# Attention epilogue two groups behind instead of one, and two constant loads issued by ScalarE

## The reference

```python
q1, k1, q2, k2, v = (heads(x @ w.T) for w in (q1_w, k1_w, q2_w, k2_w, v_w))
attn1 = softmax(q1 @ k1.T / sqrt(128));  attn2 = softmax(q2 @ k2.T / sqrt(128))
o = (attn1 - lam * attn2) @ v                      # per head, lam is one number for a head
x = layernorm(x + merge_heads(o) @ o_w.T)
scale = max(absmax(x, per token), 1e-7) / 127;  q = clip(round(x / scale), -128, 127)
f = (q @ weight.T) * scale * w_scale + bias        # weight is int8; f is rounded to f16
out = layernorm(x + f)
```

## Time and profile before

| | us |
|---|---|
| median of 3 runs (3500.14 to 3505.44) | 3500.18 |
| the profiled execution's own time | 3496.5 |
| its span, slowest core (core 4) | 3495.0 |
| spans of the 8 cores | 3478.9 to 3495.0 |
| attention block, about | 0 to 2864 |
| output projection block, about | 2865 to 3195 |
| FFN block, about | 3195 to 3495 |

### The profile page before, as it was taken

The page is one execution under the profiler, slowest core; times in us unless marked ns, Lnnn a source line. Parts: engine busy times, 40 slices in busy tenths (PEclk is TensorE's granted clock), DMA queues, the critical chain, the costliest instruction groups (busy, mean ns, idle before and its releaser), DMA issues. The chain is left out here.

```text
span 3495.0 us, 44882 instructions; the slowest of 8 cores (3478.9 to 3495.0 us)
## 1 busy us (share of the span) xinstructions
PE 3029.3 (87%) x16387; PEld 1385.5 (40%) x16640; DVE 1278.8 (37%) x1521; ACT 1268.4 (36%) x1283; POOL 36.0 (1%) x72
## 2 busy tenths in 40 slices
PE   1973999999999999898999999999999968883897
PEld 1432343434343535353535344444434323441343
DVE  0121333332323232424233323243333334774476
ACT  0250343443435251616171616152534342331222
POOL 0000000000000000000000000000000000000000
PEclk9996999999999999999999999999999988996898
DMA  9653101010101010101011010101000014443343
GB/s 149 146 175 107 34 4 34 4 34 4 34 4 35 3 35 2 35 3 36 12 27 27 11 32 5 32 6 32 6 3 5 4 61 143 122 120 115 103 123 111
DMA packets 98707, 172.79 MB, mean 49 GB/s; under 512 B 73664, under 2 KB 73664, under 8 KB 92096
## 3 DMA queue, kind: packets, MB, share of 16 engines
q0 software_dynamic: 11280, 75.50, 10.6%
q1 hardware_dynamic: 87216, 94.41, 8.6%
HBM read 174.07 MB, written 50.33 MB: 64 GB/s over the span
## 5 line engine op out<-in xcount | busy, mean ns | idle before, releaser
L279 ACT ACTIVATE pb<-psA 128x1024 bf16<-128x1024 f32 x512 | 524.2, 1024 | 1378.5 <-PE psA L243 1378.5
L261 PE MATMUL pS<-pb,ones 128*128 128x512 bf16 x2000 | 601.3, 380 | 2.5
L279 ACT ACTIVATE pb<-psB 128x1024 bf16<-128x1024 f32 x512 | 524.3, 1024 | 134.6 <-PE psB L243 134.6
L257 PE MATMUL pO<-pb,vv 128*128 128x512 bf16 x1008 | 381.1, 378 | 127.2 <-ACT pb L279 115.9
L43 DVE RECIPROCAL r<-sc_ 128x512 f32<-128x512 f32 x128 | 429.1, 3353 | 102.2 <-DMA osc<-oout 88.2
L225 PE MATMUL psB<-xTb,wq 128*128 128x512 bf16 x2000 | 460.4, 379 | 2.5
L225 PE MATMUL psA<-xTb,wq 128*128 128x512 bf16 x2000 | 457.8, 379 | 2.7 <-issue 0.2
L43 DVE COPY sc_<-pS 128x1024 f32<-128x1024 f32 x64 | 78.4, 1224 | 902.9 <-PE pS L261 902.8
L257 PE MATMUL pO<-pb,v 128*128 128x512 bf16 x1024 | 388.0, 379 | 3.7 <-issue 3.6
L243 PE MATMUL psA<-q,k 128*128 128x512 bf16 x992 | 299.9, 381 | 19.6 <-DVE k L43 17.9
L257 PEld LDWEIGHTS pO<-pb,vv 128*128 128x128 bf16 x1024 | 98.4, 96 | 517.0 <-issue 508.8
(11 more groups left out here) (73 smaller groups left out, 1734.7 us busy)
## 6 DMA issues: line engine op xcount, KB each, us to landing
wq<-wqkv POOLq DMA_DIRECT2D x16, 2560.0 KB, 16.5
xin<-x SPq DMA_DIRECT2D x16, 1024.0 KB, 5.3
out<-oo SPq DMA_DIRECT2D x16, 1024.0 KB, 5.3
xTb<-xT POOLq DMA_DIRECT2D x1, 8192.0 KB, 55.0
stg<-wo POOLq DMA_DIRECT2D x16, 512.0 KB, 6.7
wob<-stg SPq DMA_DIRECT2D x16, 512.0 KB, 2.7
stg<-wffn POOLq DMA_DIRECT2D x16, 512.0 KB, 4.7
wfb<-stg SPq DMA_DIRECT2D x16, 512.0 KB, 2.9
```

The lines of the kernel that those rows point to most:

```text
L257: te.matmul(pO[:, j * 512:(j + 1) * 512], vv[:, cc * 128:(cc + 1) * 128], pslc, start=(cc == 0), stop=(cc == NC_ - 1))
L261: mm = te.matmul(pS[:, j * 512:(j + 1) * 512], ones_sb[:], pslc, start=(cc == 0), stop=(cc == NC_ - 1))
L279: sc.activation(pb_sb[:, (c % 2) * 1024:(c % 2) * 1024 + 1024], sbank[c % 2][:], AF.Exp, scale=INV_SQRT_HD,).then_inc(sEXP, 1)
```

## The change

oc and sc_ get three parts of 1024 columns instead of two. In the loop over groups VectorE runs `divide(grp - 2)` where it ran `divide(grp - 1)`, and both last divides come behind the loop. ScalarE's copy to oc waits for the divide of three groups before instead of two. oout keeps its two halves, and the wait on sODMA inside `divide` is as it was. In the FFN block the loads of wsb_sb and bb_sb, with the wait between them, go from SP's queue to the front of ScalarE's, whose first load waits for the end of the output projection's matmuls (sAR).

```diff
-            oc_sb = Eb(nc.sbuf_tensor("oc", [128, 2048], F32))
-            sc_sb = Eb(nc.sbuf_tensor("sc_", [128, 2048], F32))
+            oc_sb = Eb(nc.sbuf_tensor("oc", [128, 3072], F32))
+            sc_sb = Eb(nc.sbuf_tensor("sc_", [128, 3072], F32))
...
-                    if grp >= 2:
-                        sc.wait_ge(sCB, grp - 1)
-                    sc.copy(oc_sb[:, (grp % 2) * 1024:(grp % 2) * 1024 + 1024],
+                    if grp >= 3:
+                        sc.wait_ge(sCB, grp - 2)
+                    sc.copy(oc_sb[:, (grp % 3) * 1024:(grp % 3) * 1024 + 1024],
...
                 def divide(g2):
-                    b2 = (g2 % 2) * 1024
+                    b2 = (g2 % 3) * 1024
                     ve.wait_ge(sOC2, g2 + 1)
                     if g2 >= 2:
                         ve.wait_ge(sODMA, 64 * (g2 - 1))
...
                         grp = h * QT + qt
-                        if grp >= 1:
-                            divide(grp - 1)
+                        if grp >= 2:
+                            divide(grp - 2)
                         ve.wait_ge(sPVD, NC_ * (grp + 1))
-                        b = (grp % 2) * 1024
+                        if grp >= 3:
+                            ve.wait_ge(sCB, grp - 2)
+                        b = (grp % 3) * 1024
                         ve.tensor_copy(sc_sb[:, b:b + 1024], pS[:], inc=(sOC, 1, grp + 1))
+                divide(H * QT - 2)
                 divide(H * QT - 1)
...
                     sy.wait_ge(sTRE, 2 * NT)
-                    sy.wait_ge(sAUX, 16)
-                    sy.dma_start(out=wsb_sb[:], in_=wsb_d).then_inc(sAUX, 16)
-                    sy.wait_ge(sAUX, 32)
-                    sy.dma_start(out=bb_sb[:], in_=bb_d).then_inc(sAUX, 16)
                     sy.wait_ge(sCS, 32 * NC_)
...
                 def _(sc):
+                    sc.wait_ge(sAR, 2 * NT)
+                    sc.wait_ge(sAUX, 16)
+                    sc.dma_start(out=wsb_sb[:], in_=wsb_d).then_inc(sAUX, 16)
+                    sc.wait_ge(sAUX, 32)
+                    sc.dma_start(out=bb_sb[:], in_=bb_d).then_inc(sAUX, 16)
```

## The result

The changed kernel takes 3436.8 us (median of 8 runs, 3435.3 to 3438.9). Its ratio to the kernel before is 0.982, 95% interval 0.981 to 0.983. The forecast was 3429, range 3420 to 3439: right in sign and inside the range, 7.8 us too low.

A forecast was written before the change was run, and what follows sets the result against it. TensorE was taken as the bound, stalled once through VectorE's wait on oout's writes. Core 7: 3420.5 without the stall, + 9.3 tail - 4.0 loads = 3425.8; with 1.5 beyond the span and about half of 3.7, 3429 us, range 3420 to 3439.

The forecast's parts named there:

- Part 1: Attention, divide two groups behind: VectorE's stall on group 0's writes goes, 78.2 us on core 4, 67.8 on core 7.
- The slack rule: Attention, behind divide(2): writes of oout could come 21 us late before TensorE noticed, 5.7 us ahead plus 15.28 idle.
- The 61 waits: Attention, ScalarE's copy of pO: with the cover gone, waits of some hundredths of a microsecond, 1 to 3 us together.
- Part 2: End of attention: two divides instead of one behind the last group, nothing hides the second, +9.3 us.
- Part 3: FFN block start: wsb_sb and bb_sb on ScalarE's queue let wfsb start earlier, gain 4.0 us, ends 0.6 and 6.8.
- What I added for the median: Whole kernel: about half of the 3.7 us by which the median of runs exceeded the profiled one.
- 3.4 us for the loads: Upward range term, FFN block: the loads get in each other's way fully, gaining 0.6 us instead of 4.0.
- The 3 us for issue: Upward range term, attention: up to 3 us if ScalarE's waits for older divides cost issue time.
- A: FFN block: loads get in each other's way fully, gain only 0.6 us, time 3432; chance 0.12.
- B: Attention, group 4: the wait returns because writes land later; 40 us late leaves a 19 us stall, 3448; chance 0.04.
- C: Attention: TensorE's stall stays because something else, such as the weights, is late too; 3505 us; chance 0.02.
- D: Attention: slower, since without the stall's rest the granted clock falls; at 0.96 the time is 3531; chance 0.02.

The follow-up runs named there:

- the experiment on late writes: The changed kernel with eight more chunks (first 8 of the FFN weight again) staged ahead of the writes of oout: 3469.6 to 3470.5 us.

## Why the prediction was right, and by how much it was not

- **Part 1 is shown.** The stall was one wait on two reused halves of oout: it is gone with the lag, and just as much with four parts and no lag. Its price, 78.2 us on core 4 with the slow clock behind it and 65 to 72 on the others, was right to within 0.4 us in the block's mean. The slack rule (a late divide costs only what exceeds the idle time behind it) held in the experiment on late writes. There the slack behind the divide measured 15.0 us, where the prediction had 15.28; the rest of its 21 us is the margin ahead of the divide. The 61 waits that might have cost 1 to 3 us leave no trace in this mean.
- **Part 2 is shown.** The tail costs 9.3 us on the timeline, and attention ends 10.6 us apart in the two kernels that differ in it. The change gives back about a seventh of what it gains here, and four parts of oout do not.
- **Part 3 had the right sign and the wrong size.** The step that failed is "One more megabyte beside it costs 2.8: gain 6.8 - 2.8 = 4.0 us". Both terms were off. The 6.8 was core 4's; the eight cores had 5.4 to 7.1, mean 6.1. And the price of the extra megabyte was above 2.8: parts 0 and 1 together took 13.2 us in the mean, 3.7 more than before (part 0 took 6.2 to 8.1, where 5 to 6 was forecast). So the last part landed 2.0 us earlier in the mean (63.1 us after the block's start, 65.2 before). Core 4 went from 66.0 to 63.2, but core 7, from which the forecast was summed, from 63.9 to 64.4. The rest of the block was another 0.6 longer. The measured gain is 1.1 to 2.4 us. The Trainium skill (DMA: Bandwidth & Descriptors, "Issuing engines are not separate DMA queues") has the transfers share the same DMA engines whatever engine issues them, and only the time to issue is saved. As the prediction worked it out, that rule gives about 0.6 us; the traces lie between it and my sum.
- **The output projection block was taken as constant.** The prediction worked out each core's time by sliding the rest of its timeline, and so put this block's growth at nothing, for which it gave no reason. It measured +3.6 us in the mean: 1.4 up to the first tile's last sum and 2.0 in the 15 distances between tiles, both places where TensorE waits for loads. Sorted by kernel, the mean of the block is 334.0 to 336.1 us in the four profiles with the lag that leave this block alone, and 331.6 to 332.4 in the four without it. The cores of the kernels with four parts enter as close together as those of the lag alone, so the growth goes with the lag and not with their nearness. It is one profile for each kernel, a pattern and not a proof, and how the lag reaches this block is open.
- **What the 7.8 us are.** The FFN block (2.6) and this block (3.6), less 0.4 in attention, make 5.8 us of the mean core, and the spread of the cores takes the slowest to 8.0. What I added for the median was 1.7 and measured 1.5.
- **The range held in part by luck.** Upward it had 3.4 us for the loads, of which most came. The 3 us for issue didn't, and the 3.6 of the output projection block, for which it had no term, took that room.
- **The rivals.** A (the loads in each other's way, 0.6 us) and the forecast's 4.0 both missed the 1.1 to 2.4 measured. B and C did not come, and D fell with the clock at 0.99 to 1.00.

What stays open: what in the pair makes ocol slower for the later core. The Trainium skill (Trainium Kernel Development and Optimization, "NeuronCore Architecture") lists 24 GiB of HBM per pair of cores. The pattern goes by pairs, but no run here counts the traffic of both cores. One exception stands too: in the changed kernel cores 4 and 5 entered 0.2 us apart and the earlier one lost 6.6 us.

## What to carry to other kernels

When one long wait stands on a reused buffer, try more of the buffer itself before delaying its user: here two more parts of 128 x 512 gave the whole gain without the tail that a longer lag leaves. Ask of every queue what its head waits for, since loads that stand behind a write of results start when the results are ready and not when their own buffer is free; moving one write was worth some 20 us. And give a block that the change doesn't touch a term in the range: here such a block moved by 3.6 us in the mean, and its slowest core by more.

## What the runs showed of the hardware

With one 512 KB load in flight at a time, the DMA engines moved 166 to 180 GB/s at a share of 0.49 to 0.53; with four in flight, 316 GB/s at 0.92. A 512 KB load that began beside a 1 MB load took 5.5 to 8.1 us, where most of the others took 3.1 to 3.5.

The version that beats both kernels has four parts of oout with divide one group behind, both constant loads on ScalarE's queue, wo loaded in attention, four loads of wfsb in flight, and the writes of ysc on POOL's queue: 3344.3 to 3344.7 us, 0.957 of the kernel before and 92 us below the changed one.
